# Attention's operations of one gated cross-attention block, listed per batch in a new order over ten pipeline steps

## The chip, the cores and the metric

The kernel runs on one core of a Trainium2 chip. The metric is the device time of one execution in microseconds, the median of several runs. A core has four compute engines, each with its own instruction queue that runs in order: PE (matmul), DVE (vector), ACT (scalar and activation) and POOL (general purpose; here it also issues the scattered row transfers). SP issues most other transfers. Engines wait for one another through semaphores only.

## The reference

```python
x = x + tanh(g_xattn[0]) * xattn(layernorm(x), ctx)   # x: 64 batches x 128 tokens x 128
x = x + tanh(g_ffn[0])   * ffn(layernorm(x))

# xattn: 16 heads of 8, ctx: 64 x 77 x 96
q, k, v = x @ Wq + bq, ctx @ Wk + bk, ctx @ Wv + bv
attn = softmax(clip(q @ k.T * 8**-0.5, -10000, 10000))
out  = (attn @ v) @ Wo + bo

# ffn: 32 experts of 128 hidden, the best 4 for each token, and a shared expert
top, idx = top_k(softmax(flat @ router_w.T + router_bias), 4)
out = sum_k(top_k / sum(top)) * down_k(silu(gate_k(flat)) * up_k(flat))
out = out + (silu(flat @ sgate_w.T) * (flat @ sup_w.T)) @ sdown_w.T
```

## The kernel before

The program has three parts. First a software pipeline goes over the 64 batches; it does the attention and the routing of each batch, and scatters the batch's 128 x 4 rows (the normalised token, its destination number and its gate) into `x_rows` in DRAM, sorted by expert. Then 288 tiles of 128 rows go through their experts (`moe`, `xin`, `y_rows`), and at the end the results are added up. The change touches the pipeline and nothing behind it.

The pipeline (`pipeline`, L231) calls a function `step(i, u, has)` on each engine, with i from -2 to 66. Batch m = i + k is at stage k in step i, and `has(k)` asks whether that batch exists. Steps -2 to 3 and 60 to 66 are written out, the 56 between run in a loop of four steps. Within a step each engine does its operations in the order in which the code lists them, for batches i+2 (first layer norm) down to i-3 (routing and scatter): a batch takes six steps.

For a batch, in order of the data. DVE takes the statistics of x (`st1`, `mv1`), POOL makes `xc` and `xn`, PE turns it and computes the queries `qT`. PE computes keys and values, DVE spreads them block-diagonally (`kvbd`, L686). PE computes the scores of 16 heads in four matmuls of 308 columns (L975) into four banks of PSUM, two halves with a signal each; there is one set of these banks. DVE takes the maxima of each half (`maxima`, L675, a 128x616 reduction each), clamps them (`mxc`) and subtracts (`difference`, L720, two halves into `prob`). The next scores wait for both differences. ACT applies a relu (L487, 128x512, and L492 the tails), PE turns the result in three fills, ACT takes the exponential (`pT`, L499), PE multiplies with the values (`context`). DVE divides (`rden`, `o_sb`, L662), PE turns `o_sb` and multiplies by Wo (L1008), DVE adds the residual (L730, into `x_all`).

Then the second norm: statistics and moments on DVE (L739, L750), the inverse deviation on ACT, and on DVE the write of the normalised rows into `payload` (L760, 128x512: four copies of the token side by side, one for each of the four rows to scatter). `payload` has two sets, batch m uses set m mod 2, and the write waits until the scatter of batch m-2 has landed (`sent`). PE turns the first copy (L983), ACT copies it out twice (`x2T`, `x2T_all`), PE computes the router's logits (L989). DVE finds the four largest (L692 to L701), casts the indices (`idxf`, L706), writes `onehot`; PE counts the tokens of each expert (L1019), DVE makes `pos` and the running `base` (L745), POOL multiplies (`prod`, L434), DVE sums (`slotf`, L765) and casts (`slot`, L771). POOL casts the destination numbers into `payload` (L440), advances them (`dest`, L443), and issues four indirect DMAs (L447), one for each of the four rows of a token.

On DVE, `slotf`, the gates and `slot` of batch i-3 are the last operations of a step and stand right behind `payload` of batch i-2.

Of the kernel before, what the change touches and what calls it, by code (L numbers as in the profile page):

```python
# [49 lines left out]
DEEP = 3  # L50
UNIT_AT = (1, 5, 9, 13)
# [5 lines left out]
    0, 128, 256, 384, 416, 448, 469, 473, 477, 478, 479, 483, 491, 499)  # L57
# [4 lines left out]
GH = 4  # L62
# [9 lines left out]
def build(nc, x, ctxT, wkv, wts, vecs, consts, experts, out):  # L72
# [4 lines left out]
    with ExitStack() as stack:  # L77
# [6 lines left out]
        def sems(name, n=2):  # L84
# [52 lines left out]
        idxf = sb("idxf", [128, TOPK])  # L137
# [8 lines left out]
        dest = sb("dest", [128, 2, TOPK])  # L146
# [48 lines left out]
        names = ("st1_d mv1_d lv1_d rs1_d xc_d xn_d xnT_p xnT_d kv_p kv_d q_p q_d vt_p vt_d s_p mx_d mxc_d diff_d relu_d "  # L195
                 "pt_p pt_d pv_p rden_d on_d oT_p oT_d y_p xb_d x1_d st2_d mv2_d lv2_d rs2_d x2_d x2T_p x2T_d x2Ta_d "
                 "lg_p lg_d top_d ntop_d idx_d idxf_d oh_d pre_p pos_d base_d prod_d slotf_d slot_d e4_d "
                 "rse_d gate_d pidx_d dest_d")
        S = {n: sem(n) for n in names.split()}
        (st1_d, mv1_d, lv1_d, rs1_d, xc_d, xn_d, xnT_p, xnT_d, kv_p, kv_d, q_p, q_d, vt_p, vt_d, s_p, mx_d, mxc_d, diff_d,  # L200
         relu_d, pt_p, pt_d, pv_p, rden_d, on_d, oT_p, oT_d, y_p, xb_d, x1_d, st2_d, mv2_d, lv2_d, rs2_d,
         x2_d, x2T_p, x2T_d, x2Ta_d, lg_p, lg_d, top_d, ntop_d, idx_d, idxf_d, oh_d, pre_p, pos_d, base_d, prod_d,
         slotf_d, slot_d, e4_d, rse_d, gate_d, pidx_d, dest_d) = S.values()
# [74 lines left out]
        def padding(first):  # L278

            return (x_rows[bass.ds(first, 128), :].rearrange("(p r) d -> p (r d)", r=8),  # L280
                    x_rows[DUMMY:DUMMY + 128, :].rearrange("(p r) d -> p (r d)", r=8))

# [117 lines left out]
        def _(pool):  # L400
            pool.wait_ge(s_cst, 16)
            nc.gpsimd.tensor_copy(dest[:, 1, :], cst[:, C_DEST:C_DEST + TOPK]).then_inc(s_dest0, 1)
# [6 lines left out]

            def step(i, u, has):  # L410
                o = 1 - u
                if isinstance(i, int) and i in (-2, 0, 3):
                    for q in {-2: (0,), 0: (1,), 3: (2, 3)}[i]:
                        pool.wait_ge(s_x[q], 16)
                if has(0):

                    need_first(pool, xn_d, i + 1)
                    xi = x_all[:, bass.ds(i * D, D)]
                    nc.gpsimd.tensor_tensor(xi, xi, bias2[:, :], ALU.add).then_inc(xb_d, 1)
                if has(2):  # L420
                    m = i + 2
                    need(pool, rs1_d, m + 1)
                    need(pool, xnT_p, m - 1)
                    need_first(pool, xn_d, m)
                    nc.gpsimd.tensor_tensor(xc[:, :], x_all[:, bass.ds(m * D, D)],
                                            mv1[:, u, 0:1].broadcast_to([128, D]), ALU.subtract).then_inc(xc_d, 1)
                    need(pool, xc_d, m + 1)
                    nc.gpsimd.tensor_tensor(xn[:, u, :], xc[:, :], rs1[:, u:u + 1].broadcast_to([128, D]),
                                            ALU.mult).then_inc(xn_d, 1)
                if has(-3):  # L430
                    m, v = i - 3, o

                    need(pool, pos_d, m + 1)
                    nc.gpsimd.tensor_tensor(prod[:, :, :], onehot[:, :, :],  # L434
                                            pos[:, :].unsqueeze(1).broadcast_to([128, TOPK, E]),
                                            ALU.mult).then_inc(prod_d, 1)

                    need(pool, sent[v], upto(m, v, 64))
                    need_first(pool, dest_d, m)
                    nc.gpsimd.tensor_copy(payload[:, v, :, D:D + 1].rearrange("p k o -> p (k o)").bitcast(U32),  # L440
                                          dest[:, 1 - v, :]).then_inc(pidx_d, 1)
                    need(pool, pidx_d, m + 1)
                    nc.gpsimd.tensor_tensor(dest[:, v, :], dest[:, 1 - v, :], cst[:, C_STEP:C_STEP + TOPK],  # L443
                                            ALU.add).then_inc(dest_d, 1)
                    need_first(pool, slot_d, m + 1)
                    for k in range(TOPK):
                        nc.gpsimd.indirect_dma_start(  # L447
                            x_rows, bass.IndirectOffsetOnAxis(ap=slot[:, v, k:k + 1], axis=0),
                            payload[:, v, k, :], None).then_inc(sent[v], 16)
# [21 lines left out]
        def _(act):  # L471
# [7 lines left out]

            def step(i, u, has):  # L480
                o = 1 - u


                def relu(n):
                    p = prob[:, u, 2 * n:2 * n + 2, 0:128 * CH]
                    need(act, diff_d, 2 * i + n + 1)
                    nc.scalar.activation(p, p, ACT.Relu, scale=-1.0).then_inc(relu_d, 1)  # L487

                def relu_tails():
                    need(act, diff_d, 2 * i)  # L490
                    need(act, pt_p, FILLS * (i - 1))
                    nc.scalar.activation(ptail[:, o, :, 0:TAIL], prob[:, o, :, 128 * CH:GK], ACT.Relu,  # L492
                                         scale=-1.0).then_inc(relu_d, 1)

                def fill(f):
                    n = 4 if f < FILLS - 1 else NG // 2
                    need(act, pt_p, FILLS * (i - 1) + f + 1)
                    need(act, pv_p, FILLS * (i - 2) + f + 1)
                    nc.scalar.activation(pT[:, f, 0:n, :].rearrange("p a b -> p (a b)"), ps_p[:, 0:n * T], ACT.Exp,  # L499
                                         scale=-1.0).then_inc(pt_d, 1)  # L500

                if has(-1):
                    relu_tails()
                if has(2):
                    m = i + 2
                    need(act, mv1_d, m + 1)
                    need(act, xn_d, m - 1)
                    nc.scalar.activation(lv1[:, u:u + 1], mv1[:, u, 1:2], ACT.Ln, bias=eps[:, :]).then_inc(lv1_d, 1)
                    need(act, lv1_d, m + 1)
                    nc.scalar.activation(rs1[:, u:u + 1], lv1[:, u:u + 1], ACT.Exp, scale=-0.5).then_inc(rs1_d, 1)  # L510
                if has(-1):
                    fill(0)
                if has(1):
                    need(act, xnT_p, i + 2)
                    need(act, q_p, i)
                    nc.scalar.copy(xnT[:, o, :], ps_f[:, 0:T]).then_inc(xnT_d, 1)
                if has(-2):
                    need(act, oT_p, i - 1)
                    need(act, y_p, i - 2)
                    nc.scalar.copy(oT[:, :], ps_b[:, 0:T]).then_inc(oT_d, 1)  # L520

                if has(-3):
                    need(act, ntop_d, i - 2)
                    need(act, gate_d, i - 3)
                    nc.scalar.activation(e4[:, :], top[:, 0:TOPK], ACT.Exp, bias=ntop[:, :],
                                         accum_out=se4[:, :]).then_inc(e4_d, 1)
                if has(-1):
                    fill(1)
                if has(1):
                    need(act, q_p, i + 2)  # L530
                    need(act, s_p, 2 * i)
                    nc.scalar.activation(qT[:, o, :], ps_f[:, 0:T], ACT.Identity, bias=bq_s[:, :],
                                         scale=HD ** -0.5).then_inc(q_d, 1)
                if has(0):
                    relu(0)
                if has(-2):
                    need(act, mv2_d, i - 1)
                    need(act, x2_d, i - 2)
                    nc.scalar.activation(lv2[:, :], mv2[:, 1:2], ACT.Ln, bias=eps[:, :]).then_inc(lv2_d, 1)
                if has(-1):  # L540
                    fill(2)
                if has(-2):
                    need(act, lv2_d, i - 1)
                    nc.scalar.activation(rs2[:, :], lv2[:, :], ACT.Exp, scale=-0.5).then_inc(rs2_d, 1)
# [665 lines left out]
```

## Time and profile before

| | |
|---|---|
| runs (device time, us) | 1058.04 and 1057.62, median 1057.83 |
| the profiled execution (us) | 1048.59, its span 1046.8 |
| busy in the span | PE 87%, DVE 70%, POOL 64%, ACT 52% |
| mean granted clock of PE | 0.953 of full speed |
| the pipeline | first scatter at 48.4 us, last one begins to be issued at 571.3 us |
| the chain that ended last, its largest parts | transfers into `x_rows` 12%, their issue on POOL 10% |

A timeline row gives the start, the duration, the engine, the line, the operation with its tiles, and in brackets the idle time of the engine ahead of it with what ended it. The records of one engine overlap a little, since an engine begins the next operation while the last one drains. What an operation costs in a row of others is therefore read from start to start.

### The profile page before, as it was taken

Reading aid. Unit: us, or ns where it says so; the run is one execution under the profiler, and the core shown is the slowest. Engines: PE = TensorE matmul, PEld = TensorE weight load, DVE = VectorE, ACT = ScalarE, POOL = GpSimd, SP = SyncE. Lnnn points to the kernel's source line nnn. Section 1 sums busy time; section 2 is a strip of 40 time slices with the busy share of each in tenths; the row PEclk is TensorE's granted clock in tenths of the full one; section 3 lists DMA queues with packets and bytes.
Section 4 is the critical chain, followed back from the end, with each engine's and each line's share of the span. In section 5 each row is a group of like instructions: output and inputs, shape, how many; then the busy total and the mean of one; then the engine's idle time right before and its main releaser. Section 6 shows DMA issues by size and latency. Waiting matters only on the chain.

```text
span 1046.8 us, 27382 instructions
## 1 busy us (share of the span) xinstructions
PE 906.9 (87%) x6880; PEld 743.1 (71%) x6880; DVE 737.8 (70%) x2490; ACT 542.7 (52%) x1925; POOL 670.5 (64%) x937
## 2 busy tenths in 40 slices
PE   4988888888888888988895599989899899899785
PEld 2777777777777677777673478878888788789453
DVE  3788888988888898888785245645555455456498
ACT  3666677777766776777662234434434344344111
POOL 1267777777676777777665177777777776777300
PEclk9999999999999999999986789989999899899998
DMA  5111111111111111111212687788888887877497
GB/s 151 49 36 38 34 37 34 37 37 39 34 34 34 37 37 37 37 34 34 64 37 74 184 266 239 231 250 248 239 257 254 246 251 228 245 241 211 140 391 272
DMA packets 129108, 140.77 MB, mean 134 GB/s; under 512 B 25868, under 2 KB 110457, under 8 KB 129074
## 3 DMA queue, kind: packets, MB, share of 16 engines
q1 hardware_dynamic: 111090, 105.41, 34.0%
q0 software_dynamic: 17472, 33.87, 9.2%
q10 hardware_dynamic: 512, 1.07, 0.5%
q8 instruction: 17, 0.28, 0.1%
q14 instruction: 17, 0.14, 0.0%
HBM read 102.18 MB, written 42.31 MB: 138 GB/s over the span
## 4 chain that ended last, share of the span: by engine, by line
PE 31%; issue 18%; DMA 16%; DVE 16%; POOL 11%; SPq 6%; POOLq 1%; ACT 0%; DVEq 0%; ACTq 0%
DMA x_rows<-payload,slot 12%; POOL x_rows L447 10%; PE ps L1088 5%; PE ps L1080 4%; PE ps L1082 4%; PE ps L1098 4%; PE ps L1114 3%; DVE payload L760 3%; PE ps L1104 3%; PE ps L1073 2%; DVE kvbd L686 2%; SPq L274 2%; DVE moe L889 2%; DMA y_rows<-y_sb,xin 2%; SPq L338 1%
## 5 line engine op out<-in xcount | busy, mean ns | idle before, releaser
L461 POOL DMA_INDIRECT y_rows<-y_sb,xin x288 | 283.2, 983 | 119.7 <-issue 68.6
L447 POOL DMA_INDIRECT x_rows<-payload,slot x256 | 251.3, 982 | 134.1 <-DVE slot L771 71.9
L592 ACT ACTIVATE sg<-ps 128x128 f32<-128x128 f32 x288 | 79.9, 278 | 149.2 <-PE ps L1082 144.6
L851 DVE TENSOR_SCALAR y_sb<-ps,xin 128x128 f32<-128x128 f32 x288 | 100.0, 347 | 75.3 <-PE ps L1088 72.6
L845 DVE TENSOR_TENSOR hT<-sg,ps 128x128 f32<-128x128 f32 x288 | 82.9, 288 | 95.4 <-ACT sg L592 91.8
L950 PE MATMUL ps<-vt,pT 128*128 128x108 f32 x1024 | 144.0, 285 | 0.0
L950 PEld LDWEIGHTS ps<-vt,pT 128*128 128x128 f32 x1024 | 128.9, 197 | 11.3 <-issue 11.1
L1088 PE MATMUL ps<-moe,hT 128*128 128x128 f32 x576 | 120.9, 293 | 2.7 <-DVE hT L845 1.9
L587 ACT COPY xT<-ps 128x128 f32<-128x128 f32 x288 | 75.4, 262 | 85.5 <-PE ps L1073 85.4
L1080 PE MATMUL ps<-xT,moe 128*128 128x128 f32 x576 | 115.7, 284 | 0.0
L1082 PE MATMUL ps<-xT,moe 128*128 128x128 f32 x576 | 115.6, 284 | 0.0
L487 ACT ACTIVATE prob<-prob 128x512 f32<-128x512 f32 x128 | 80.5, 630 | 62.2 <-DVE prob L720 60.7
L1088 PEld LDWEIGHTS ps<-moe,hT 128*128 128x128 f32 x576 | 89.6, 196 | 29.7 <-DVE hT L845 26.3
L675 DVE TENSOR_REDUCE mx<-ps 128x8 f32<-128x616 f32 x128 | 101.1, 790 | 4.3 <-PE ps L975 3.9
L499 ACT ACTIVATE pT<-ps 128x512 f32<-128x512 f32 (+1 forms) x192 | 99.8, 520 | 6.1 <-PE ps L927 5.0
L1073 PE MATMUL ps<-cst,xin 128*128 128x128 f32 x288 | 82.8, 287 | 23.1 <-DMA xin<-x_rows 22.4
L720 DVE SCALAR_TENSOR_TENSOR prob<-ps,mxc 128x616 f32<-128x616 f32 x128 | 99.5, 779 | 0.1
L1082 PEld LDWEIGHTS ps<-xT,moe 128*128 128x128 f32 x576 | 91.6, 200 | 0.0
L1080 PEld LDWEIGHTS ps<-xT,moe 128*128 128x128 f32 x576 | 91.6, 200 | 0.0
L927 PE MATMUL ps<-cst,prob 128*128 128x128 f32 x512 | 81.5, 283 | 0.3 <-ACT pT L499 0.3
L1073 PEld LDWEIGHTS ps<-cst,xin 128*128 128x128 f32 x288 | 41.9, 146 | 46.4 <-DMA xin<-x_rows 26.1
L994 PE MATMUL ps<-cst,xn 128*128 128x128 f32 x64 | 21.6, 337 | 59.5 <-DVE kvbd L686 59.5
(136 smaller groups left out, 1933.5 us busy)
## 6 DMA issues: line engine op xcount, KB each, us to landing
moe<-in_experts SPq DMA_DIRECT2D x288, 192.0 KB
xin<-x_rows SPq DMA_DIRECT2D x288, 65.0 KB
moe<-y_rows SPq DMA_DIRECT2D x16, 1024.0 KB, 8.9
y_rows<-y_sb,xin POOLq DMA_INDIRECT x288
x_rows<-payload,slot POOLq DMA_INDIRECT x256, 2.4
out<-x_all SPq DMA_DIRECT2D x16, 256.0 KB, 6.5
ctx_sb<-in_ctxT SPq DMA_DIRECT2D x64, 29.2 KB
x_rows<-x_rows ACTq DMA_DIRECT2D x16, 65.0 KB, 2.6
```

What stands on the lines that cost most here:

```text
L447: nc.gpsimd.indirect_dma_start(x_rows, bass.IndirectOffsetOnAxis(ap=slot[:, v, k:k + 1], axis=0), payload[:, v, k, :], None).then_inc(sent ...
L461: nc.gpsimd.indirect_dma_start(y_rows, bass.IndirectOffsetOnAxis(ap=xin[:, u, D:D + 1].bitcast(U32), axis=0), y_sb[:, u, :], None, bounds_ ...
L499: nc.scalar.activation(pT[:, f, 0:n, :].rearrange("p a b -> p (a b)"), ps_p[:, 0:n * T], ACT.Exp, scale=-1.0).then_inc(pt_d, 1)
L675: nc.vector.reduce_max(mx[:, 2 * GH * n:2 * GH * (n + 1)].rearrange("p (g a) -> p g a", a=GH), ps[:, 2 * n:2 * n + 2, 0:GK].rearrange("p g ...
L720: nc.vector.scalar_tensor_tensor(out=prob[:, u, 2 * n:2 * n + 2, :].rearrange("p g (a k) -> p g a k", a=GH), in0=ps[:, 2 * n:2 * n + 2, 0: ...
L845: nc.vector.tensor_tensor(hT[:, u % DEEP, :], sg[:, u % DEEP, :], ps_gu[u % 2][:, H:2 * H], ALU.mult).then_inc(hT_d[u % PER], 1)
L851: nc.vector.tensor_scalar(y_sb[:, u % U3, :], ps_dn[u % 2][:, 0:D], xin[:, u % U3, D + 1:ROW], None, ALU.mult).then_inc(y_d[u % PER], 1)
L950: r = nc.tensor.matmul(ps_o[:, at:at + 3 * GC], pT[:, f, n, :], vt[:, o, c, near:near + 3, :].rearrange("p g c -> p (g c)"), start=f == 0 ...
L1073: after(nc.tensor.transpose(ps_xT[:, 0:128], xin[:, u % U3, 0:D], ident), xin_in, n16, u).then_inc(xT_p[u % PER], 1)
L1080: after(nc.tensor.matmul(ps_gu[u % 2][:, 0:H], w_t[:, u % U3, 0:H], xT[:, u % 2, :], start=True, stop=True), xT_d, n, u)
L1082: nc.tensor.matmul(ps_gu[u % 2][:, H:2 * H], w_t[:, u % U3, H:2 * H], xT[:, u % 2, :], start=True, stop=True).then_inc(gu_p[u % PER], 1)
L1088: after(nc.tensor.matmul(ps_dn[u % 2][:, 0:D], hT[:, u % DEEP, :], w_t[:, u % U3, 2 * H:EW], start=True, stop=True), hT_d, n, u).then_inc( ...
```

## The change

The pipeline becomes ten steps deep (batches i+2 to i-7); -2 to 11 are written out, 48 steps run in the loop, and 60 to 71 are written out. Every operation is a small function of its batch, and each engine's step lists them in a new order.

- DVE: the step begins with `kvbd` of batch i-1 and the second maxima of batch i-2, and the chain of the routing of batch i-7 stands between them and the second difference. `slot` of batch i-7 comes ahead of the first difference of batch i-2, which is now behind the second. Behind it come `o_sb` (i-4), the residual (i-5), the normalised rows (i-6), and at the end the first maxima of batch i-1.
- The normalised rows are written once (128x128); ACT copies them three times into the other rows of the set (`copies`, 128x384).
- The cast `idxf` is gone, `onehot` compares with the integer indices.
- POOL keeps the destination number in the payload and adds two batches' worth to it (`next_index`); `dest` is gone. `product` and `next_index` stand at the start of POOL's step.
- PE: the scores of batch i-1 stand between the turn of `o_sb` and the projection of batch i-5. They wait for both differences of batch i-2.
- ACT: the relu and exponential of the first half belong to batch i-3, of the second to i-2 and i-3.

The number of sets of `payload` is two in both kernels.

```diff
+FIRST, LAST, FULL = -2, 8, 12
-            for i in range(-2, 4):
+            for i in range(FIRST, FULL):
                 step(i, i % 2, lambda k, i=i: 0 <= i + k < B)
-            with eng.Fori(1, B // 4 - 1) as j:
+            with eng.Fori(FULL // 4, B // 4 - 1) as j:
                 for u in range(4):
                     step(4 * j + u, u % 2, lambda k: True)
-            for i in range(B - 4, B + 3):
+            for i in range(B - 4, B + LAST):
...
+            def next_index(m, v):
+                need(pool, sent[v], upto(m, v, 64))
+                need_first(pool, pidx_d, m - 1)
+                field = payload[:, v, :, D:D + 1].rearrange("p k o -> p (k o)").bitcast(I32)
+                nc.gpsimd.tensor_tensor(field, field, two_steps[:, :], ALU.add).then_inc(pidx_d, 1)
...
+            def scatter_rows(m, v):
+                need(pool, pidx_d, m + 1)
+                need(pool, copies_d, m + 1)
+                need_first(pool, slot_d, m + 1)
...
+                if has(-7):
+                    product(i - 7)
+                    next_index(i - 7, o)
                 if has(2):
+                    centered(i + 2, u)
+                    normed(i + 2, u)
+                if has(-2):
+                    biased(i - 2)
+                if has(-7):
+                    scatter_rows(i - 7, o)
...
+            def copies(m, v):
+                need(act, x2_d, m + 1)
+                nc.scalar.copy(payload[:, v, 1:TOPK, 0:D],
+                               payload[:, v, 0:1, 0:D].broadcast_to([128, TOPK - 1, D])).then_inc(copies_d, 1)
...
+            def residual(m):
+                xm = x_all[:, bass.ds(m * D, D)]
+                need(dve, y_p, m + 1)
+                need(dve, xb_d, m + 1)
...
+            def normed2(m, v):
+                need(dve, rs2_d, m + 1)
+                need(dve, sent[v], upto(m, v, 64))
+                nc.vector.tensor_scalar(payload[:, v, 0, 0:D], x_all[:, bass.ds(m * D, D)],
+                                        mv2[:, 0:1], rs2[:, :], ALU.subtract, ALU.mult).then_inc(x2_d, 1)
...
+            def scores(m, v):
+                need(pe, q_d, m + 1)
+                need(pe, kv_d, m + 1)
+                need(pe, diff0_d, m)
+                need(pe, diff1_d, m)
...
+            def projected(m):
+                need(pe, oT_d, m + 1)
+                nc.tensor.matmul(ps_b[:, 0:D], oT[:, :], w[:, W_O:W_O + D], start=True, stop=True).then_inc(y_p, 1)
```

DVE's queue before, in the pipeline, around the write of the payload (from the second `difference` of a step to `kvbd` in the next):

```order
L720 SCALAR_TENSOR_TENSOR prob<-ps,mxc 128x616
L755 RECIPROCAL rse<-se 128x1
L760 TENSOR_SCALAR payload<-x_all,mv,rs 128x4x128
L765 TENSOR_REDUCE slotf<-prod 128x4
L768 TENSOR_SCALAR payload<-e,rse,tg 128x4
L771 CAST slot<-slotf 128x4
```

`slot`, for which POOL's transfers wait, stands behind the write of the payload. After the change, on the same engine, from `pos` to `kvbd` of the next step:

```order
L799 TENSOR_TENSOR pos<-ps,base 128x32
L800 TENSOR_TENSOR base<-ps,base 128x32
L805 RECIPROCAL rse<-se 128x1
L762 BN_AGGR mv<-st 128x2
L809 TENSOR_SCALAR payload<-e,rse,tg 128x4
L814 TENSOR_REDUCE slotf<-prod 128x4
L737 RECIPROCAL rden<-ps 128x16
L818 CAST slot<-slotf 128x4
L727 SCALAR_TENSOR_TENSOR prob<-ps,mxc 128x616
L743 TENSOR_TENSOR o_sb<-ps,rden 128x128
L753 SCALAR_TENSOR_TENSOR x_all<-ps,tg,x_all 128x128
L768 TENSOR_SCALAR payload<-x_all,mv,rs 128x128
```

`slot` has moved ahead of the payload's write (L768, now 128x128), and between them stand a difference, `o_sb` and the residual. On PE, before, from the scores (L975) of a step to its projection (L1008):

```order
L975 MATMUL ps<-kvbd,qT 128x308 x4
L983 MATMUL ps<-cst,payload 128x128
L965 MATMUL ps<-ctx_sb,wkv_sb 128x77 x2
L927 MATMUL ps<-cst,prob 128x128 x4
L989 MATMUL ps<-w,x2T 128x32
L994 MATMUL ps<-cst,xn 128x128
L998 MATMUL ps<-cst,o_sb 128x128
L927 MATMUL ps<-cst,prob 128x128 x4
L1004 MATMUL ps<-xnT,w 128x128
L1008 MATMUL ps<-w,oT 128x128
```

After the change, on PE, from the turn of `o_sb` (L1106) over the scores (L1058) and the projection (L1110) to the router (L1123):

```order
L1106 MATMUL ps<-cst,o_sb 128x128
L1058 MATMUL ps<-kvbd,qT 128x308 x4
L1110 MATMUL ps<-w,oT 128x128
L1070 MATMUL ps<-cst,prob 128x128 x4
L1031 MATMUL ps<-ctx_sb,wkv_sb 128x77 x2
L1118 MATMUL ps<-cst,payload 128x128
L1092 MATMUL ps<-vt,pT 128x108 x4
L1076 MATMUL ps<-cst,ptail 128x128 x2
L1123 MATMUL ps<-w,x2T 128x32
```

The projection stood nine entries behind the scores and now stands right behind them; the router's matmul stands in the step after the turn of the payload, behind four matmuls of the context and two turns of the tails.

## Rows read from the trace of the kernel before

**Rows 1.** Busy time by engine, 400 to 500 us (PE, PEld, DVE, ACT, POOL, clock, DMA, GB/s).

```profile
400.00:500.00 100.00, 88.29 (x791) 74.03 (x791) 88.24 (x329) 70.82 (x242) 73.32 (x122) 0.99 0.11 36
```

**Rows 2.** The chain that ended last, 327 to 341 us: start, duration, what.

```profile
330.08 0.55 DVE payload L760
...
331.91 1.04 POOL x_rows L447
...
335.79 2.28 DMA x_rows<-payload,slot
...
338.10 0.64 DVE payload L760
...
340.02 1.04 POOL x_rows L447
```

**Rows 3.** Waits, 100 to 500 us: us in total, times, longest.

```profile
DVE rden L654 <- issue: 3.2, 12, 0.3
```

**Rows 4.** Timeline of POOL: a scatter's first transfer for four of the batches.

```profile
48.39 1.19 POOL L447 DMA_INDIRECT x_rows<-payload,slot  x1 [1.33 <-DVE slot L771]
...
530.88 1.04 POOL L447 DMA_INDIRECT x_rows<-payload,slot  x1 [1.28 <-DVE slot L771]
...
561.25 1.04 POOL L447 DMA_INDIRECT x_rows<-payload,slot  x1 [1.86 <-DVE slot L771]
...
567.41 1.04 POOL L447 DMA_INDIRECT x_rows<-payload,slot  x1 [0.46 <-DVE slot L771]
```

**Rows 5.** Timeline of DVE through one step of the loop, 497 to 505 us.

```profile
497.12 0.18 DVE L692 TENSOR_TENSOR lg<-ps,vec 128x32 f32<-128x32 f32 x1
497.48 0.20 DVE L698 MAX8 top<-lg 128x8 f32<-128x32 f32 x1 [0.18 <-DVE lg L692]
...
498.65 0.16 DVE L706 CAST idxf<-idx 128x4 f32<-128x4 uint32 x1
498.77 0.17 DVE L710 TENSOR_SCALAR mxc<-mx 128x16 f32<-128x16 f32 x1
...
499.34 0.79 DVE L720 SCALAR_TENSOR_TENSOR prob<-ps,mxc 128x616 f32<-128x616 f32 x1
500.05 0.29 DVE L739 BATCH_NORM_STATS2 st<-x_all 128x6 f32 x1
...
502.02 0.64 DVE L760 TENSOR_SCALAR payload<-x_all,mv,rs 128x512 f32 x1 [0.60 <-DMA x_rows<-payload,slot]
502.58 0.28 DVE L765 TENSOR_REDUCE slotf<-prod 128x4 f32<-128x128 f32 x1
...
503.36 0.26 DVE L662 TENSOR_TENSOR o_sb<-ps,rden 128x128 f32<-128x128 f32 x1
503.59 0.18 DVE L670 BATCH_NORM_AGGREGATE mv<-st 128x2 f32<-128x6 f32 x1
...
505.13 0.18 DVE L692 TENSOR_TENSOR lg<-ps,vec 128x32 f32<-128x32 f32 x1
```

**Rows 6.** Timeline of PE: a projection, and scores with what follows them.

```profile
534.34 0.39 PE L1008 MATMUL ps<-w,oT 128*128 128x128 f32 x2
...
538.16 0.80 PE L975 MATMUL ps<-kvbd,qT 32*128 32x308 f32 x8
538.89 0.33 PE L983 MATMUL ps<-cst,payload 128*128 128x128 f32 x1
```

**Rows 7.** Timeline of POOL between two scatters: in the loop, and behind it.

```profile
338.03 0.42 POOL L434 TENSOR_TENSOR prod<-onehot,pos 128x128 f32<-128x128 bf16 x1
338.40 0.38 POOL L440 CAST payload<-dest 128x4 uint32<-128x4 f32 x1
...
558.92 0.19 POOL L440 CAST payload<-dest 128x4 uint32<-128x4 f32 x1
```

**Rows 8.** Timeline of DVE at the start of the pipeline: the first batch's clamp.

```profile
21.64 0.18 DVE L710 TENSOR_SCALAR mxc<-mx 128x16 f32<-128x16 f32 x1
```

**Rows 9.** Groups by line and shape, 100 to 500 us: count, busy, mean ns, idle before.

```profile
L499 ACT ACTIVATE pT<-ps 128x512 f32<-128x512 f32 x98 | 58.5, 597 | 1.1 <-PE ps L927 0.4
```

More of the change, by code:

```diff
@@ L430, in step @@
[L430 to L449, printed above, removed]
@@ L511, in step @@
[L511 to L516, printed above, removed]
+                if has(-7):
+                    evacuate_x2T(i - 7)
+                    copies(i - 7, o)
+                if has(-3):
+                    relu(i - 3, o, 0)
+                if has(0):
+                    evacuate_xnT(i, u)
+                if has(-4):
+                    fill(i - 4, 2)
@@ L522, in step @@
                 if has(-3):
[L523 to L533, printed above, removed]
@@ L565, in _ @@
+                if has(-3):
+                    fill(i - 3, 1)
+                    relu_tails(i - 3, o)
             pipeline(act, step)
@@ new lines, in gates, with slot_sums, slots @@
+            def gates(m, v):
+                need(dve, rse_d, m + 1)
+                nc.vector.tensor_scalar(payload[:, v, :, D + 1:ROW].rearrange("p k o -> p (k o)"), e4[:, :],
+                                        rse4[:, :], tg[:, 1:2], ALU.mult, ALU.mult).then_inc(gate_d, 1)
+            def slot_sums(m):
+                need(dve, prod_d, m + 1)
+                nc.vector.reduce_sum(slotf[:, :], prod[:, :, :], AX_X).then_inc(slotf_d, 1)
+            def slots(m, v):
+                need(dve, slotf_d, m + 1)
+                nc.vector.tensor_copy(slot[:, v, :], slotf[:, :]).then_inc(slot_d, 1)
@@ new lines, in step @@
+                if has(-7):
+                    positions(i - 7, o)
+                    inverse_sum(i - 7)
+                if has(-6):
+                    moments2(i - 6)
+                if has(-7):
+                    gates(i - 7, o)
+                    slot_sums(i - 7)
+                if has(-4):
+                    reciprocals(i - 4)
+                if has(-7):
+                    slots(i - 7, o)
+                if has(-2):
+                    difference(i - 2, u, 0)
+                if has(-4):
+                    attended(i - 4)
@@ L773, in _ @@
+                if has(-5):
+                    residual(i - 5)
+                if has(-6):
+                    normed2(i - 6, u)
+                if has(-1):
+                    maxima(i - 1, 0)
             pipeline(dve, step)
@@ new lines, in scores @@
+            def scores(m, v):
+                need(pe, q_d, m + 1)
+                need(pe, kv_d, m + 1)
+                need(pe, diff0_d, m)
+                need(pe, diff1_d, m)
+                for g in range(NG):
+                    rows = slice(GH * HD * g, GH * HD * (g + 1))
+                    r = nc.tensor.matmul(bank[g][:, 0:GK], qT[rows, v, :],
+                                         kvbd[rows, v, 0, :, :].rearrange("p a k -> p (a k)"), start=True,
+                                         stop=True)
+                    if g % 2:
+                        r.then_inc(s_p, 1)
@@ new lines, in context @@
+            def context(m, v, f):
+                need(pe, pt_d, FILLS * m + f + 1)
+                if f == 0:
+                    need(pe, vt_d, m + 1)
+                    need(pe, on_d, m)
+                if f < FILLS - 1:
+                    for n in range(4):
+                        g, c = divmod(4 * f + n, CH)
+                        near = min(max(g - 1, 0), NG - 3)
+                        at = g * GS - (g - near) * GC
+                        r = nc.tensor.matmul(ps_o[:, at:at + 3 * GC], pT[:, f, n, :],
+                                             vt[:, v, c, near:near + 3, :].rearrange("p g c -> p (g c)"),
+                                             start=f == 0 and n == 0, stop=False)
+                else:
+                    for n in range(NG // 2):
+                        r = nc.tensor.matmul(ov[:, 2 * n:2 * n + 2, 0:GC], pT[:, f, n, :], vtail[:, v, n, :, :],
+                                             start=False, stop=n == NG // 2 - 1)
+                r.then_inc(pv_p, 1)
@@ new lines, in router, with counted @@
+            def router(m):
+                need(pe, x2T_d, m + 1)
+                need(pe, x2Ta_d, m + 1)
+                nc.tensor.matmul(ps_b[:, 0:E], x2T[:, :], w[:, W_R:W_R + E], start=True,
+                                 stop=True).then_inc(lg_p, 1)
+            def counted(m):
+                need(pe, oh_d, m + 1)
+                for n, lhs in enumerate((tri, ones)):
+                    for k in range(TOPK):
+                        r = nc.tensor.matmul(ps_b[:, n * E:(n + 1) * E], lhs[:, :], onehot[:, k, :],
+                                             start=k == 0, stop=k == TOPK - 1)
+                r.then_inc(pre_p, 1)
@@ L980, in step @@
[L980 to L984 removed]
+                if has(-4):
+                    context(i - 4, u, 0)
+                    turn(i - 4, u, 2)
+                if has(-7):
+                    router(i - 7)
+                if has(0):
+                    turn_x1(i, u)
+                if has(-4):
+                    context(i - 4, u, 1)
```

589 lines of the change are left out of this document (295 added, 294 removed).

## The prediction

> **What bounds the kernel now.** I read the busy times by stretch first. In a steady 100 us of the pipeline PE and DVE are each busy 88% and POOL 73%, at full clock [rows 1]. Nobody is full, so some chain of waits sets the step. The chain that ended last shows it: write of the payload on DVE, slot, four scattered transfers on POOL, the landing of the last one, and then the next write of the payload, 8.02 us after the one before [rows 2]. DVE's timeline shows the same from its side: in a step of 8.01 us (from one `lg` to the next) it is idle for 0.60 us ahead of the payload, released by the landing, and for 0.18 us ahead of `MAX8` [rows 5]. There are two payload sets, yet the ring closes in one step. The slot of a batch stands in DVE's order behind the payload of the next batch, and this payload needs the set whose transfers have just landed. So each scatter waits for the landing of the scatter before it.
>
> From the first batch's scatter to the last one's are 519.0 us and 63 gaps. The last five gaps, where the pipeline drains, take 36.5 us; the 58 ahead of them take 482.5 us, 8.32 each [rows 4]. A steady gap is 8.11 (331.91 to 340.02 [rows 2]). The excess of 0.2 on average I put down to stretches at a low clock and to the loop's edges, and leave it as it is.
>
> **The change, part by part.**
>
> *The ring.* With the slot ahead of the payload's write, the payload of batch m waits for the landing of m-2 and its slot comes one step later. The new ring is at most one step from payload to slot, and then the old ring without the payload's own 0.55, which is 7.47 [rows 2]. At a step of 7.9 that makes 15.4, and it may take two steps, 15.8. It no longer sets the step, with some 0.4 to spare at least, and DVE loses the idle 0.60.
>
> *DVE's work.* The step of 8.01 minus both idle times (0.78; `MAX8` now has statistics between it and `lg`) minus `idxf`, 0.12 from start to start, minus the narrower payload. This took 0.56 from start to start; a 128x128 operation, `o_sb`, takes 0.23. The 128x128 write has no row; it lies between `idxf`'s 0.12 (four columns) and this 0.23, and I take 0.20, nearest to the equal shape, so 0.36 less. 8.01 - 0.78 - 0.12 - 0.36 = 6.75 us of work [rows 5].
>
> *The new wait.* The first difference now stands late, and behind it in the order `o_sb` and the residual. The residual needs the projection, PE has the projection behind the scores, and the scores wait for this same difference. Count from the start of the difference: its record is 0.79 [rows 5], the hop to PE about 0.03 (a landing at 338.07 released the payload at 338.10 [rows 2]), the scores occupy PE for 0.73 until the next matmul starts, the projection's record is 0.39 [rows 6], another hop 0.03: the residual can start at 1.97. DVE reaches it after the difference (0.71) and `o_sb` (0.23), at 0.94 [rows 5]. **So DVE stands still for about 1.03 us in every step.** What is queued behind it is the normalised write and the first maxima; the maxima need the scores, which are done by then. The stall can't be below 0.9 unless scores or projection are shorter than their rows. It is this wait that eats the gain.
>
> *Smaller waits.* `slotf` needs POOL's product (0.42 [rows 7]) after `pos`; between the two DVE has `base`, two small operations and the gates, about 0.5 in all, against 0.42 and two hops: 0 to 0.1, I take 0.05. The loop's edge costs DVE 3.2 us in 400 us, 0.07 a step [rows 3]. Together 6.75 + 1.03 + 0.05 + 0.07 = **7.90 us a step** against 8.11: a gain of 0.21 at most times.
>
> *What is moved to ACT.* A copy of 128x384 costs more than nothing and less than a 128x512 exponential, 0.597 [rows 9]; I take 0.5, nearest to the wide row. On an engine that is busy 71% [rows 1] it is hidden, since ACT then has some 6.2 of 7.9; without that cover it would cost up to 0.6 a step. The scatter waits for the copies too, but they stand at the start of ACT's step and the slot late in DVE's.
>
> *POOL.* Four issues take 3.88 from the first to the last and about 0.96 more [rows 2]; with product, three 128x128 operations of about 0.4 and the index it has some 7 us of 7.9. The destination cast takes 0.19 alone behind the loop, and 0.38 in the loop, where it ends together with DVE's payload of 0.64 [rows 2, 7]. The Trainium skill ("SBUF — State Buffer", "SBUF: two separate sides") says that a DVE operation in a two-port mode and a GpSimd operation lock the port pair they share for a whole instruction; the trace agrees with a block of 0.19. This gives a rival, below.
>
> *Fill and drain.* The first batch is clamped at 21.64 [rows 8] in step 0 before and in step 2 after. Its scatter comes in step 7: five steps and some 3.1 us later. The 3.1 is an estimate from the order: `onehot`, one difference of 0.71 and eight small operations of 0.1 to 0.2 [rows 5] up to the slot, and 0.8 to the first transfer. A filling step is at least the loop of two maxima, `kvbd` and two differences at 0.71 each [rows 5] with the scores' 0.73 [rows 6] and a few small ones, about 5.0, and at most a full one, 7.9; I take the middle, 6.4. So 21.6 + 32 + 3.1 = 56.7 against 48.4 [rows 4]: **8.3 later**, bounds 1.3 and 16. The drain has six gaps now; before, the last gap took 6.16 and the others up to 7.6 [rows 4]. Payload and slot no longer alternate in the ring, so I take 6.2, near the last; 7.6 would cost 8 more.
>
> *Sum, for the profiled execution (1048.6, 9.2 below the median).* 57 full gaps at 8.32 - 0.21 make 462.3, six drain gaps 37.2: 499.5 against 519.0, so -19.5. With +8.3 for the fill the net is -11. The rest of the program starts from the last slot and is unchanged. 1057.8 - 11 = **1047**.
>
> **Rivals.**
>
> *The engines become the bound.* If the residual's wait were covered, DVE would need 6.87, and POOL's 7 us or a little more would set a step of 7.3: -0.6 more in 57 gaps, -34, so 1013. For it: the work is there to be overlapped. Against: in-order queues leave nothing for DVE to do ahead of the residual. The Trainium skill ("Perfetto Trace Analysis", "Identifying the Most-Contended Engine") tells to judge by the engine with the highest occupancy, which by [rows 1] is DVE with PE; that would give this rival. Chance 0.13.
>
> *The router's chain comes late; slower than before.* The normalised write ends about 2.4 after the difference; PE turns it, ACT copies it, PE must do the context and tail matmuls before the router, and `lg` is due on DVE 2.1 later. By the order this has about 0.2 to spare. If the copy stands behind one exponential of 0.597 [rows 9], `lg` and everything behind it on DVE is late by up to 0.4 a step. From 0.19 a step (11 us in 57 gaps) the whole gain is gone; at 0.4 it is 23 us more, 1070. Chance 0.16.
>
> *The shared port.* `slot` and the normalised write could be held by a POOL operation of 0.42 that runs beside them [rows 7]; `slot` stands where POOL does its three 128x128 operations. Up to 0.42 a step, 24 us: 1071. Against: the small cast `idxf` has a record of no more than 0.16 [rows 5]. Chance 0.08.
>
> *The change doesn't undo the ring.* If the slots still waited for the last landing, the step stays 8.1, and with the fill and the shorter drain 1047 + 12 = 1059. The ring's slack is thin, but [rows 2] counts it with the payload twice. Chance 0.07.
>
> **How the numbers follow.** My forecast, a step of 7.7 to 8.1, has 0.52 and spans 1036 to 1059; 0.04 is left for what I don't see. The range, 1022 to 1068, leaves out most of the engine-bound case and the ends of the slow ones. About 2% (21 us) can be told from no change here: faster is under 1036.7, which has the engine-bound case 0.13 and a tenth to a fifth of the forecast, 0.23 together; slower is over 1079, 0.06, the two slow rivals with a late fill; the same, 0.71.
>
> **What would show it.** Right: in the loop DVE idle for about 1.0 us ahead of the residual, released by PE's projection, no idle time ahead of the payload from a landing, gaps between scatters of 7.9, the first scatter near 57. Wrong: gaps under 7.5 (the residual finds its projection done), or DVE idle ahead of `lg`, `slotf` or `rden` for more than 0.2, or first scatter beyond 65.

## The result, and the profile after

The changed kernel took 1069.51 us (1069.21 and 1069.80) against 1057.83 before, a ratio of 1.0123, interval 1.0089 to 1.0156. The kernel before varies by itself: its runs lie between 1045.7 and 1058.0 over all comparisons. Measured side by side in alternation, the change gave 1067.80 against 1051.45, **ratio 1.0149 (1.0123 to 1.0174)**. I had said 1047 and a gain of 1%; it is a loss of 1.2 to 1.5%, within the 2% that count as the same.

Busy shares fell in the steady stretch; nothing became full [against rows 1].

```profile
400.00:500.00 100.00, 84.04 (x753) 68.93 (x752) 81.64 (x308) 68.42 (x248) 66.76 (x107) 1.00 0.11 34
```

POOL's timeline after: the first batch's first transfer, then those of five successive batches in the loop. The first comes 15.1 us later than in [rows 4], and the gaps are 8.91, 8.34, 8.33 and 8.41 (the same four over and over), a mean of 8.50 against the steady 8.11 of [rows 2].

```profile
63.51 1.17 POOL L453 DMA_INDIRECT x_rows<-payload,slot  x1 [0.17 <-issue]
...
403.85 1.01 POOL L453 DMA_INDIRECT x_rows<-payload,slot  x1 [0.17 <-issue]
...
412.76 1.01 POOL L453 DMA_INDIRECT x_rows<-payload,slot  x1 [0.26 <-issue]
...
421.10 1.01 POOL L453 DMA_INDIRECT x_rows<-payload,slot  x1 [0.17 <-issue]
...
429.43 1.01 POOL L453 DMA_INDIRECT x_rows<-payload,slot  x1 [0.17 <-issue]
...
437.84 1.01 POOL L453 DMA_INDIRECT x_rows<-payload,slot  x1 [0.17 <-issue]
```

DVE's timeline after, from `slot` to the first maxima, the part that answers to the payload's wait in [rows 5]:

```profile
402.63 0.19 DVE L818 CAST slot<-slotf 128x4 uint32<-128x4 f32 x1
402.73 0.79 DVE L727 SCALAR_TENSOR_TENSOR prob<-ps,mxc 128x616 f32<-128x616 f32 x1
403.44 0.28 DVE L743 TENSOR_TENSOR o_sb<-ps,rden 128x128 f32<-128x128 f32 x1
405.15 0.35 DVE L753 SCALAR_TENSOR_TENSOR x_all<-ps,tg,x_all 128x128 f32 x1 [1.44 <-PE ps L1110]
405.42 0.34 DVE L768 TENSOR_SCALAR payload<-x_all,mv,rs 128x128 f32 x1
405.67 0.79 DVE L716 TENSOR_REDUCE mx<-ps 128x8 f32<-128x616 f32 x1
```

PE's timeline in the same place (turn of `o_sb`, scores, projection):

```profile
402.23 0.33 PE L1106 MATMUL ps<-cst,o_sb 128*128 128x128 f32 x1
403.77 0.80 PE L1058 MATMUL ps<-kvbd,qT 32*128 32x308 f32 x8 [1.21 <-DVE prob L727]
404.51 0.49 PE L1110 MATMUL ps<-w,oT 128*128 128x128 f32 x2
```

The residual waits for the projection (L1110), which waits behind the scores (L1058), which wait for the late difference (L727): the chain that was forecast, at the place that was forecast. PE stands idle 1.21 us ahead of the scores and DVE 1.44 ahead of the residual, in every step. The waits over 400 us (us in total, times, longest) hold the same two, and none of the payload for a landing any more:

```profile
DVE x_all L753 <- PE ps L1110: 69.1, 47, 2.2
...
PE ps L1058 <- DVE prob L727: 57.7, 47, 1.3
```

### The profile page after: what moved, and what is told of

The parts are those of the page before. It is cut to its first block, busy times and chain, and to the rows that moved or that the text cites. A ratio compares the mean times of both kernels' runs of the same rounds, so it can differ in the third digit from the quotient of the medians.

```text
span 1068.0 us, 27041 instructions
## 1 busy us (share of the span) xinstructions
PE 902.9 (85%) x6880; PEld 736.6 (69%) x6880; DVE 719.4 (67%) x2426; ACT 546.6 (51%) x1989; POOL 651.0 (61%) x875
## 4 chain that ended last, share of the span: by engine, by line
PE 33%; DVE 30%; issue 17%; SPq 11%; DMA 4%; POOL 3%; DVEq 1%; ACT 0%; POOLq 0%
DVE prob L727 5%; PE ps L1058 5%; PE ps L1220 4%; DVE kvbd L708 4%; PE ps L1212 4%; PE ps L1214 4%; SPq L342 4%; DVE mx L716 3%; SPq L345 3%; PE ps L1246 3%; PE ps L1230 3%; PE ps L1236 3%; PE ps L1110 2%; SPq L276 2%; POOL x_rows L453 2%
## 5 line engine op out<-in xcount | busy, mean ns | idle before, releaser
L1092 PE MATMUL ps<-vt,pT 128*128 128x108 f32 x1024 | 136.2, 276 | 3.3 <-issue 3.2
L1058 PE MATMUL ps<-kvbd,qT 32*128 32x308 f32 x512 | 54.6, 495 | 72.0 <-DVE prob L727 72.0
L727 DVE SCALAR_TENSOR_TENSOR prob<-ps,mxc 128x616 f32<-128x616 f32 x128 | 100.9, 790 | 0.5 <-DVE mxc L722 0.3
L537 ACT ACTIVATE prob<-prob 128x512 f32<-128x512 f32 x128 | 81.7, 639 | 21.2 <-DVE prob L727 20.9
L444 POOL TENSOR_TENSOR prod<-onehot,pos 128x128 f32<-128x128 bf16 x64 | 27.3, 426 | 95.9 <-DVE pos L799 95.8
```

The costliest lines, as they stand in the source:

```text
L727: nc.vector.scalar_tensor_tensor(out=prob[:, v, 2 * n:2 * n + 2, :].rearrange("p g (a k) -> p g a k", a=GH), in0=ps[:, 2 * n:2 * n + 2, 0: ...
L1058: r = nc.tensor.matmul(bank[g][:, 0:GK], qT[rows, v, :], kvbd[rows, v, 0, :, :].rearrange("p a k -> p (a k)"), start=True, stop=True)
L1092: r = nc.tensor.matmul(ps_o[:, at:at + 3 * GC], pT[:, f, n, :], vt[:, v, c, near:near + 3, :].rearrange("p g c -> p (g c)"), start=f == 0 ...
```

## The experiments

A ratio under 1 is faster. Two theories stood against each other. A: the step is set by this one chain, late difference, scores, projection, residual, and goes with it. B: depth, copies or POOL set it, and the idle time only shows there. All ratios are against the kernel before, run beside them.

**The kernel before, again.**

> The kernel before, unchanged, to get a second profile: its first profiled execution (1048.6) was 9.2 us below the median of its runs, the one after is at its median (1069.8 against 1069.5). If the 9 us lie in the pipeline, the scatters' gaps here are 0.1 to 0.2 longer than the 8.11 of the first profile; if they lie behind it (expert tiles, PE's clock there), first to last scatter is 519 us again and the span differs behind 590 us. If the first profile was an ordinary one, this run is near 1048 or 1058 by chance and the two levels are the kernel's own spread.

1056.1, with first to last scatter 521.9 against 519.0, 2.0 us more ahead of it and 2.7 behind it. The profile I had predicted from was one of the faster ones of a kernel that varies by 1%; I keep to ratios.

**The projection ahead of the scores** (in the changed kernel, PE):

```diff
-                if has(-1):
-                    scores(i - 1, o)
                 if has(-5):
                     projected(i - 5)
+                if has(-1):
+                    scores(i - 1, o)
```

> The changed kernel with one swap on PE: the projection of batch i-5 ahead of the scores of batch i-1. Theory A (DVE stands still 1.5 us ahead of the residual because the projection is queued behind scores that wait for the late difference): the residual's idle time falls from 1.5 to under 0.1, a wait of 0.3 to 0.6 for the scores appears ahead of the first maxima, a step falls from 8.34 to 7.3 to 7.5, and the time by about 55 us, to 1005 to 1025. Rival B (the depth, ACT's copies or POOL hold the step and the stall is only where the slack shows): another engine's wait takes its place and the time stays over 1055.

1025.3, ratio 0.976 (0.972 to 0.980): one swap gives back 42 us, not the 55 expected. PE's and DVE's timelines of this kernel:

```profile
402.83 0.49 PE L1110 MATMUL ps<-w,oT 128*128 128x128 f32 x2 [0.64 <-ACT oT L556]
403.40 0.80 PE L1058 MATMUL ps<-kvbd,qT 32*128 32x308 f32 x8
```

```profile
403.48 0.35 DVE L753 SCALAR_TENSOR_TENSOR x_all<-ps,tg,x_all 128x128 f32 x1
403.74 0.34 DVE L768 TENSOR_SCALAR payload<-x_all,mv,rs 128x128 f32 x1
404.23 0.80 DVE L716 TENSOR_REDUCE mx<-ps 128x8 f32<-128x616 f32 x1 [0.15 <-PE ps L1058]
405.32 0.80 DVE L708 TENSOR_TENSOR kvbd<-ps,cst 128x616 f32<-128x616 f32 x1 [0.29 <-PE ps L1031]
```

The residual's idle time is gone. 0.15 and 0.29 are left: DVE waits for the scores, and then for keys and values, which stand behind the scores on PE. A step is 7.6 to 8.0, longer than the 7.3 to 7.5 expected, but nothing else has taken the stall's place. A holds, B falls.

**The first difference early** (in the changed kernel, DVE):

```diff
                     difference(i - 2, u, 1)
+                    difference(i - 2, u, 0)
...
-                if has(-2):
-                    difference(i - 2, u, 0)
                 if has(-4):
                     attended(i - 4)
```

> The changed kernel with the first half's difference right behind the second one again, all else kept: undoes the part 'first half's difference late'. Theory A: scores and projection run under DVE's small operations, the residual's idle time falls to 0 to 0.4, a step to 7.2 to 7.5, the time to 1005 to 1025. Rival B: over 1055. If the step only falls to 7.8, POOL (issues of 4.9 and five operations) has become the bound.

1018.3, ratio 0.970 (0.966 to 0.974), 49 us under the changed kernel. A step is 7.4 to 7.6, and 8.1 at the loop's edge; 0.45 are left ahead of the residual:

```profile
406.04 0.35 DVE L753 SCALAR_TENSOR_TENSOR x_all<-ps,tg,x_all 128x128 f32 x1 [0.45 <-PE ps L1109]
```

So the one part "first half's difference late" turned a gain of 3% into a loss of 1.5%.

**Both, with keys and values ahead of the second turn** (the two edits above, and on PE):

```diff
+                if has(0):
+                    keys_values(i, u)
                 if has(-3):
                     turn(i - 3, o, 1)
-                if has(0):
-                    keys_values(i, u)
```

> Both cures, and the wait that the swap on PE brought out (kvbd for keys and values, 0.3 us): first difference early, projection ahead of the scores, keys and values ahead of the turn of the second half. Theory A: the residual's 0.45 idle of the early difference goes; DVE needs 6.9 a step and POOL about 7.2, so a step of 7.1 to 7.4 and 1000 to 1012 us. If the scores now come later than DVE's first maxima, as much is lost there and the time stays at 1015 to 1025.

1050.1, ratio 0.998 (0.996 to 1.000), outside both outcomes that I had expected. The two cures with the third edit lose what each cure gained alone. The chain of waits of this kernel, at its middle:

```profile
407.00 0.30 ACT lv L561
...
407.44 0.26 ACT oT L556
...
407.74 0.49 PE ps L1109 x2
408.23 0.73 PE ps L1057 x8
408.96 0.60 PE ps L1030 x4
409.56 0.44 PE ps L1069 x4
410.00 0.11 PE ps L1117
410.11 0.88 PE ps L1091 x8
...
411.46 0.30 PE ps L1122 x2
```

The projection waits for `oT` on ACT, which stands behind the second norm's deviation (`lv`), and now everything on PE up to the router (L1122) queues behind it; `lg` waits 0.57 to 0.65 for the router and closes a ring of 8.1 over one step. With one of the two cures alone a step is 7.4 to 8.1; as keys and values were moved in this kernel only, no run shows which pair of the three edits closes the ring.

**The scores' waits in the other order** (PE, below), and **one of them left out** (without `need(pe, diff1_d, m)`, which DVE's order of the two differences makes superfluous):

```diff
-                need(pe, diff0_d, m)
                 need(pe, diff1_d, m)
+                need(pe, diff0_d, m)
```

> The changed kernel with the scores' last two waits in the other order on PE (the second half's difference first, the late first half last). The scores begin 0.25 us after the difference's end; a relu on ACT begins 0.04 after it. If the 0.2 is PE's sequencer working through another wait behind the one that comes last, it falls to 0.1 or less, a step by 0.1 to 0.2 and the time by 6 to 12 us. If it belongs to the first weight load or matmul behind an empty PE, nothing changes (within 2 us).

> The changed kernel with one wait less at the scores on PE (the wait for the second half's difference, which DVE always ends before the first half's; the order is kept by the wait for the latter). The swap of the two waits gained 0.11 a step (1061). If PE's sequencer pays only for waits behind the one that comes last, this is the same as the swap, 1060 to 1063. If each wait in front costs as well, 1054 to 1059.

1061.2, ratio 1.0086 (1.0060 to 1.0112), and 1060.6, ratio 1.0095 (1.0063 to 1.0126): the same. The difference and the scores in the swapped kernel:

```profile
404.48 0.79 DVE L727 SCALAR_TENSOR_TENSOR prob<-ps,mxc 128x616 f32<-128x616 f32 x1
```

```profile
405.42 0.80 PE L1058 MATMUL ps<-kvbd,qT 32*128 32x308 f32 x8 [1.16 <-DVE prob L727]
```

From 0.25 the gap falls to 0.15 (405.42 against 404.48 + 0.79), and a step by 0.11. At the scores a wait behind the one that comes last costs 0.1 us of the chain; with it ahead or absent the time is the same. 0.15 stays; the last section reads what it is made of.

**The first maxima ahead of the residual** (in the changed kernel, DVE):

```diff
+                if has(-1):
+                    maxima(i - 1, 0)
                 if has(-5):
                     residual(i - 5)
                 if has(-6):
                     normed2(i - 6, u)
-                if has(-1):
-                    maxima(i - 1, 0)
```

> The changed kernel with the first maxima of batch i-1 ahead of the residual and the normalised write on DVE: undoes 'maxima at the step's end'. The 1.5 us idle ahead of the residual goes; the maxima then wait about 0.95 for the scores, and residual and normalised rows come 0.2 later than now. If the stall were DVE's alone, the step falls by 0.5 to 7.8 and the time to 1035 to 1045. If PE's way from the normalised rows over context and tails to the router is right behind it, DVE stands still ahead of lg for 0.5 to 0.9 instead, and the time stays at 1060 to 1072.

1065.6, ratio 1.0139 (1.0091 to 1.0186), no gain that can be told. DVE's timeline of it:

```profile
401.09 0.80 DVE L716 TENSOR_REDUCE mx<-ps 128x8 f32<-128x616 f32 x1 [0.88 <-PE ps L1058]
401.81 0.34 DVE L753 SCALAR_TENSOR_TENSOR x_all<-ps,tg,x_all 128x128 f32 x1
...
404.66 0.19 DVE L773 TENSOR_TENSOR lg<-ps,vec 128x32 f32<-128x32 f32 x1 [0.70 <-PE ps L1123]
```

The idle time ahead of the residual has become 0.88 ahead of the maxima and 0.70 ahead of `lg` at the loop's edge, where it waits for the router. The router's chain (payload, turn, context, tails, router) stood right behind the one I had counted.

**The payload written wide again** (in the changed kernel; the scatter's wait for the copies goes too):

```diff
-                nc.vector.tensor_scalar(payload[:, v, 0, 0:D], x_all[:, bass.ds(m * D, D)],
+                nc.vector.tensor_scalar(payload[:, v, :, 0:D],
+                                        x_all[:, bass.ds(m * D, D)].unsqueeze(1).broadcast_to([128, TOPK, D]),
...
-                    copies(i - 7, o)
```

> The changed kernel with the four copies of the normalised rows written by DVE in one operation again (128x512) and without ACT's copies: undoes the narrower payload alone. The narrow write takes 0.25 us from start to start here, the wide one took 0.56, and it stands behind the residual on the path that sets the step. Theory A: DVE's path grows by 0.3 a step, 58 steps give 16 to 20 us, 1082 to 1090. If PE's way from the payload to the router is what counts there, the same. If another wait sets the step at this place, less than 5 us.

1082.5, ratio 1.0305 (1.0265 to 1.0346), 15 us over the changed kernel. The gaps are 8.53 to 8.60 against 8.33 to 8.41, so the narrow write is worth about 0.2 a step here, where it lies on the chain.

**The kernel before, with the slots ahead of the payload** (DVE, alone), and then **also product and destination ahead of bias and first norm** (POOL):

```diff
+                if has(-3):
+                    m, v = i - 3, o
+                    need(dve, prod_d, m + 1)
+                    nc.vector.reduce_sum(slotf[:, :], prod[:, :, :], AX_X).then_inc(slotf_d, 1)
...
                 if has(-2):
                     m = i - 2
                     need(dve, rs2_d, m + 1)
```

```diff
+                if has(-3):
+                    m, v = i - 3, o
+                    need(pool, pos_d, m + 1)
+                    nc.gpsimd.tensor_tensor(prod[:, :, :], onehot[:, :, :],
...
                 if has(0):
                     need_first(pool, xn_d, i + 1)
```

> The kernel before with one part of the change alone: slot sums, gates and slots of batch i-3 ahead of the write of the payload of batch i-2 on DVE. If the scatter's ring was what set the step before, it falls from 8.11 to about 7.4 (DVE's work 7.2, landings 7.0 after a slot), 58 gaps give about -35 us, 1015 to 1035. If something else was close behind (the router's chain, PE's order), less than 10 us are gained.

> The kernel before with the slots ahead of the payload on DVE (step 7.97, 1033 us) and also the product and the destination ahead of the bias and the first norm on POOL. With the slots first alone, slotf waited for the product, which stood behind three operations of 0.4 us behind the last scatter: a ring on POOL of 7.97. If so, the step falls by about 0.5 to 1.0 to 7.0 to 7.5 and the time to 980 to 1010, below the ten-step versions, since the fill stays short (first scatter 48.8). If another ring is close behind (payload to router to slot), it stays over 7.7 and 1020.

The first: 1033.1, ratio 0.985 (0.980 to 0.990), a step of 7.97 and not the 7.4 expected. POOL's timeline of it, from the end of one scatter to the start of the next, and one of its waits:

```profile
400.57 0.47 POOL L419 TENSOR_TENSOR x_all<-x_all,bias 128x128 f32 x1
...
401.83 0.43 POOL L434 TENSOR_TENSOR prod<-onehot,pos 128x128 f32<-128x128 bf16 x1
...
403.67 1.05 POOL L447 DMA_INDIRECT x_rows<-payload,slot  x1 [0.99 <-DVE slot L765]
```

```profile
DVE slotf L759 <- POOL prod L434: 23.7, 49, 2.3
```

Scatter, bias, first norm, product, `slotf`, `slot`, scatter: a ring on POOL, 0.14 shorter than the old one. With the product moved it opens too: **1009.3, ratio 0.960 (0.958 to 0.962)**, a step of 7.4. This six-step kernel is faster than the kernel before and the changed one; DVE is busy 95% of its steady stretch.

**The same with the destination kept in the payload and without the cast of the indices:**

```diff
-                    nc.gpsimd.tensor_copy(payload[:, v, :, D:D + 1].rearrange("p k o -> p (k o)").bitcast(U32),
-                                          dest[:, 1 - v, :]).then_inc(pidx_d, 1)
...
+                    nc.gpsimd.tensor_tensor(field, field, two_steps[:, :], ALU.add).then_inc(pidx_d, 1)
...
-                    nc.vector.tensor_copy(idxf[:, :], idx[:, 0:TOPK]).then_inc(idxf_d, 1)
```

> The six-step kernel with slots and product moved ahead (1009 us, POOL's operations end to end at 7.4 a step) and, from the change, the destination kept in the payload (one addition for a cast and an addition on POOL) and no cast of the indices on DVE. If POOL is the bound there, its step falls by 0.1 to 0.3, and the time to 992 to 1003. If DVE or PE has become the bound, it stays within 4 us of 1009.

1011.9, ratio 0.962 (0.957 to 0.967): nothing gained. POOL's busy time falls from 78.2 to 74.0 in 100 us and a step is 7.5 against 7.4, so the amount of POOL's work does not set it. First the kernel with product and slots ahead, then this one, 250 to 350 us:

```profile
250.00:350.00 100.00, 93.78 (x845) 78.28 (x844) 95.23 (x357) 75.15 (x262) 78.22 (x132) 1.00 0.12 39
```

```profile
250.00:350.00 100.00, 92.94 (x838) 77.52 (x841) 95.25 (x339) 75.13 (x261) 73.98 (x118) 1.00 0.12 39
```

DVE stays at 95 although its cast is gone. The write of the payload has become longer, by more than 0.15 on average (150 to 450 us: total, mean ns, idle before; first the kernel with product and slots ahead, then this one):

```profile
L772 DVE TENSOR_SCALAR payload<-x_all,mv,rs 128x512 f32 x40 | 23.7, 593 | 0.7 <-DMA x_rows<-payload,slot 0.4
```

```profile
L769 DVE TENSOR_SCALAR payload<-x_all,mv,rs 128x512 f32 x40 | 29.9, 748 | 0.3 <-DMA x_rows<-payload,slot 0.3
```

Why it is longer is open. DVE is the fullest engine here, with PE at 93; that it sets the step is not shown.

## Why the prediction was wrong, step by step

**The ring opens: right.** No payload waits for a landing in the loop, so the rival that the ring stays falls, and the slots-first kernel shows that the ring was the bound before. It also shows what I had not counted: opening it alone uncovers POOL's own ring 0.14 a step below.

**The new wait: right in place and cause, wrong in size. This is the step that failed.** I counted 1.97 from the start of the difference to the residual, an idle time of 1.03. It is 2.42 (402.73 to 405.15), and from start to start the residual is 1.5 late. Term by term: the hop from DVE to PE is 0.25, not 0.03 (403.52 to 403.77); the scores 0.74, as counted; the projection's record 0.49, not 0.39 (in the trace before, 0.49 stands in the drain, at 541.18); its hop to DVE 0.15, not 0.03. Together 0.45 a step, some 26 us in 57 gaps, twice the 12 us that the whole step was to gain.

I had priced both hops with a landing that released DVE, and I set a bound below (0.9) and none above. Before, the scores never waited for a difference, but the trace did hold waits between the same engines, PE's turn of `xn` behind `kvbd`, and the residual behind the projection:

```profile
306.78 0.79 DVE L686 TENSOR_TENSOR kvbd<-ps,cst 128x616 f32<-128x616 f32 x1
307.62 0.33 PE L994 MATMUL ps<-cst,xn 128*128 128x128 f32 x1 [0.93 <-DVE kvbd L686]
```

```profile
69.30 0.63 PE L1008 MATMUL ps<-w,oT 128*128 128x128 f32 x2
70.09 0.35 DVE L730 SCALAR_TENSOR_TENSOR x_all<-ps,tg,x_all 128x128 f32 x1 [0.70 <-PE ps L1008]
```

These hops are 0.05 (307.57 to 307.62) and 0.16 (69.93 to 70.09). They would have given 0.15 of the 0.34 by which the two hops were too short; the rest lies in how PE takes its waits at the scores (last section).

**DVE's work: right.** 8.34 less 1.48 leaves 6.86; forecast 6.80 with the small waits.

**The loop's edge: too small.** I took 0.07 a step; the gaps of 8.91 and 8.41 beside 8.34 make 0.16. At the edge `lg` starts at 408.00, right behind the router's end (407.66 + 0.31), so the second chain was met there already.

**Fill: too small.** The first transfer came at 63.5, not 56.7. DVE's timeline and the chain of waits after:

```profile
26.34 0.14 DVE L722 TENSOR_SCALAR mxc<-mx 128x16 f32<-128x16 f32 x1
...
60.02 0.16 DVE L722 TENSOR_SCALAR mxc<-mx 128x16 f32<-128x16 f32 x1
```

```profile
21.19 0.80 PE ps L1022 x2
21.99 1.34 PE ps L1058 x8
```

I had kept the first clamp at 21.6, but it moved to 26.3 [rows 8]: the first batch's scores (L1058) now stand on PE behind the next batch's turn and queries (L1022), and start at 21.92 against 17.58 before. The clamp's delay is 4.7 of the 6.8. Five steps of 6.74 instead of 6.4 are 1.7, and from the clamp (60.02) to the transfer it took 3.5, not 3.1. Every ten-step variant started at 62 to 67, the six-step ones at 48 to 50. The ten-step kernels share most of their order too, and no run changes the depth alone, so the 12 to 19 us between them are not shown to be the depth's.

**Drain: too short.** Five gaps of 6.6 and one of 10.0 (8.9 in a second profile) make 43.3 against 37.2. I took one row, 6.16, for all six.

**The sum, profile against profile.** Between the profiled executions the span grew by 21.2; I had said -11. Measured less forecast: steady step and edges +21 (57 gaps at 8.47 on average against 8.32 - 0.21 = 8.11), fill +7, drain +6, behind the last scatter -1. Measured after less before it looks different: the first scatter comes 15.1 later, the 57 gaps take 9.5 more (8.47 against 8.31), the drain 2.2 less and the rest 1.3 less. So the stall ate the gain of the opened ring and 9.5 us more, and the larger part of the loss is the later start. Against medians it is less, since the profile before lay 9 us under its median.

**The rivals.** The router's chain: its 1070 is the time that came, but not its mechanism; it stood next in line, as the kernel with the maxima ahead shows. The shared port: `slot` has records of 0.12 to 0.26 in the loop, beside POOL's operations, against 0.15 to 0.17 before, and the normalised write 0.34 in every step, so no block of 0.4 is there, and the rival falls for this kernel. That the engines bind: DVE comes near to full only in the last six-step kernels, and that it binds there is not shown. Within 2% had 0.71 and came, on the side that I had not forecast; that was luck, given by the width of the band.

**The range** ended at 1068. A bound of 0.3 for each hop, seen in hindsight as just wide enough for the 0.25, would have put 2 x 0.27 x 57 = 31 us on its upper side, and the gain of 11 could not have stood as the likeliest by a wide margin.

## What to carry to other kernels

A chain that goes round several in-order engines within one step is a sum of short pieces, and each hop in it is a term like any other: price it from a row with the same two engines and the same number of waits, and where there is none, bound it above. When a ring is opened, look for the next ring with its own period before pricing the gain, here 7.97 behind 8.11. Where an operation has several waits, look for what stands between the late signal and the operation: at the scores, moving the late wait one place back in the list gave 0.1 a step. And ask of an operation that is placed late who stands behind its consumer in that consumer's queue.

## What the runs showed of the hardware

The signal itself took about 0.04 us; the rest of a hop was instructions that stood between the signal and the operation. The traces hold them, although the timelines leave them out: semaphore instructions, which do nothing but wait, and register instructions.

**From DVE to PE.** In the changed kernel the difference ends at 403.52. PE's semaphore instruction that waits for it starts at 403.56, a second one, for the other difference and `kvbd`, at 403.67, the weight load of the scores at 403.74, the first matmul at 403.77. With the two waits swapped the second instruction is done 1.6 us ahead of the signal, and from the difference's end (405.27) to the first matmul (405.42) only one is left: 0.04 to it, 0.08 from it to the weight load, 0.03 to the matmul. In all 47 steps between 100 and 500 us the hop is 0.25 or more, and in all 48 of the swapped kernel 0.15. The Trainium skill ("Perfetto Trace Analysis", "Identifying Dependency Chains") says that an instruction which waits on several engines may have separate semaphore instructions put ahead of it; the trace agrees, with two of them ahead of the scores.

The wait that the code lists first is carried by the weight load itself: at the scores that is the one for `qT`, and at the turn of `xn` in the kernel before the one for `kvbd`, the late one, and there PE starts after 0.05. Whether the scores would gain another 0.1 with the late wait listed first, no run shows.

**From PE to DVE.** In the loop the residual has a register instruction ahead of it that takes the projection's signal (405.04, behind the projection's end at 405.00), and starts 0.15 to 0.16 behind that end, before and after the change. In the steps that are written out that instruction is absent, and where the residual waits for the projection it starts after 0.04 (before: 526.18 behind 526.14).
